# A sequence buffer in chunks of eight steps with permuted PSUM writes, and the encoder's output gate on ScalarE

## The reference

```
h = tok(x)                         # q, k, v = x@W + b; scores = q k^T; y = (gamma * scores) v @ Wo + bo
                                   # h = y if y >= 0 else 0.25 * y
n = layernorm(h)                   # (16, 1024, 64)
h_fwd = lstm(n @ Wf + bf, Uf)                  # last hidden state, 128 wide
h_bwd = lstm(n @ Wb + bb, Ub, reverse=True)
dec   = lstm(concat(h_fwd, h_bwd) @ Wd + bd, Ud, return_sequences=True)   # same input at every step
h = h + dec @ Wo + bo
h = h + experts(layernorm(h))      # 8 experts, the best 2 of each token, exact gelu
```

## Time and profile before

| | |
|---|---|
| median of 3 runs | 4055.97 us (4055.7 to 4057.27) |
| the profiled execution's own time | 4059.22 us |
| its span, first to last instruction | 4057.4 us |
| mean granted TensorE clock | 0.954 of full speed |
| PE busy | 3735.3 us, 92% |
| DVE busy | 3216.8 us, 79% |
| ACT busy | 1822.8 us, 45% |
| POOL busy | 86.1 us, 2% |

### The profile page before, as it was taken

One profiled execution on the slowest core, in us unless ns is written; L12 is line 12 of the kernel. 1 busy time (PEld: TensorE's weight loads), 2 busy tenths in 40 slices (PEclk: granted clock), 3 DMA queues, 4 the chain that ended last, 5 costly groups with the idle time before them and its releaser, 6 DMA issues. The chain is left out here.

```text
span 4057.4 us, 159902 instructions
## 1 busy us (share of the span) xinstructions
PE 3735.3 (92%) x59839; PEld 2527.7 (62%) x59839; DVE 3216.8 (79%) x23274; ACT 1822.8 (45%) x9834; POOL 86.1 (2%) x131
## 2 busy tenths in 40 slices
PE   6888799999999999999999799999998999899898
PEld 3222377777777777777777655655555555555564
DVE  5766699999999999999999766767666677666775
ACT  3333355555555555555555343434444343434443
POOL 6100000000000000000000000000000000000000
PEclk8888899999999999999999799999999999999999
DMA  3000000000000000000000000000000000000000
GB/s 88 16 21 16 14 3 3 3 3 3 3 3 3 3 4 3 3 4 3 3 3 4 5 6 6 8 7 7 6 7 6 7 7 7 7 6 6 7 7 7
DMA packets 49586, 33.99 MB, mean 8 GB/s; under 512 B 37661, under 2 KB 46877, under 8 KB 48806
## 3 DMA queue, kind: packets, MB, share of 16 engines
q1 hardware_dynamic: 48806, 23.77, 2.3%
HBM read 15.37 MB, written 8.39 MB: 6 GB/s over the span
## 5 line engine op out<-in xcount | busy, mean ns | idle before, releaser
L733 PE MATMUL bank<-xs,ident 128*128 128x128 f16 x13490 | 1202.4, 222 | 0.0
L733 PEld LDWEIGHTS bank<-xs,ident 128*128 128x128 f16 x13490 | 824.4, 98 | 60.5 <-issue 38.2
L742 PEld LDWEIGHTS bank<-enc_hi,u_lo 128*128 128x128 f16 x8192 | 350.3, 98 | 321.1 <-DVE enc_hi L788 311.5
L745 PE MATMUL bank<-enc_lo,u_hi 128*128 128x16 f16 x8192 | 529.9, 173 | 10.7 <-DVE enc_lo L794 8.9
L742 PE MATMUL bank<-enc_hi,u_lo 128*128 128x16 f16 x8192 | 532.9, 173 | 5.8 <-DVE enc_hi L788 4.5
L767 DVE SCALAR_TENSOR_TENSOR terms_dec<-ifg_cell_dec 128x32 f32<-128x32 f32 x1024 | 197.4, 193 | 417.6 <-ACT ifg_cell_dec L753 407.0
L753 ACT ACTIVATE ifg_cell_dec<-bank 128x48 f32<-128x48 f32 x1024 | 216.1, 211 | 659.4 <-PE bank L745 659.4
L742 PE MATMUL bank<-enc_hi,u_hi 128*128 128x16 f16 x8192 | 502.3, 170 | 0.0
L742 PEld LDWEIGHTS bank<-ring_hi,u_lo 128*128 128x128 f16 x4096 | 175.8, 97 | 484.7 <-DVE ring_hi L788 465.5
L742 PE MATMUL bank<-ring_hi,u_lo 128*128 128x16 f16 x4096 | 264.3, 173 | 183.7 <-DVE ring_hi L788 149.8
L745 PEld LDWEIGHTS bank<-enc_lo,u_hi 128*128 128x128 f16 x8192 | 341.6, 97 | 87.7 <-DVE enc_lo L794 16.8
(11 more groups left out here) (269 smaller groups left out, 7960.9 us busy)
## 6 DMA issues: line engine op xcount, KB each, us to landing
g_rows<-tok_d_gamma_batched_dram SPq DMA_DIRECT2D x8, 512.0 KB, 6.7
x_rows<-in_x_dram SPq DMA_DIRECT2D x16, 256.0 KB, 3.1
kept_h<-tok_ln_h SPq DMA_DIRECT2D x32, 128.0 KB, 2.0
res<-kept_h SPq DMA_DIRECT2D x32, 128.0 KB
out_dram<-sums SPq DMA_DIRECT2D x32, 128.0 KB
raw_wd<-in_L_attn_Wd_dram SPq DMA_DIRECT2D x2, 256.0 KB
raw_experts<-in_L_ffn_W_dram SPq DMA_DIRECT2D x2, 256.0 KB
raw_u<-in_L_attn_Uf_dram SPq DMA_DIRECT2D x1, 256.0 KB
```

The source lines that it names most:

```text
L733: nc.tensor.matmul(spare, m.ident16[:], m.xs[:, COLS:COLS + P], start=False, stop=True, skip_group_check=True)
L742: nc.tensor.matmul(z[k], w[:, g, :], h_hi, start=False, stop=False, skip_group_check=True)
L745: last = nc.tensor.matmul(z[k], m.u_hi[c.d][:, g, :], h_lo, start=False, stop=True, skip_group_check=True)
```

## The change

- `xs` becomes (chunk of 8 steps, batch, step) without pads, so that L582 writes runs of 8 steps (16 bytes) for its batch.
- A fill reads its 128 columns as one contiguous block still, now in the order (batch, step). To put them where they belong, its output in PSUM is addressed in the order (batch, step) too: `z.rearrange("p t b -> p b t")`.
- The encoder's output gate, (tanh(o) + 1) * 0.5 * scale, moves from DVE (L779) to ACT, as an Identity activation with scale and a bias from the tile `half_scale`, right behind the tanh of o. It waits for that tanh.
- DVE's waits for `s_out_gate` (ahead of `enc_hi`) and, in the encoder, for `s_cell` (ahead of `terms`) are dropped.
- `dve_rest` stays as it was for the decoder.

```diff
--- before.py
+++ after.py
@@ -107,7 +107,7 @@
         m.gT = sb("gammaT", [P, NB, T], F32)
 
 
-        m.xs = sb("xs", [P, T * B + 2 * COLS], F16)
+        m.xs = sb("xs", [P, CHUNKS, B, STEPS], F16)
         m.u_hi = [sb(f"u_hi{d}", [P, 4, H], F16) for d in range(3)]
         m.u_lo = [sb(f"u_lo{d}", [P, 4, H], F16) for d in range(3)]
         m.w_hi = [sb(f"w_hi{d}", [P, 4, H], F16) for d in range(2)]
@@ -240,8 +240,6 @@
                 nc.gpsimd.memset(m.bias[:], 0.0).then_inc(s_bz, 1)
                 nc.gpsimd.memset(m.ones3[:], Z_SCALE)
                 nc.gpsimd.memset(m.ones_s[:], MIX_SCALE ** 2)
-                nc.gpsimd.memset(m.xs[:, 0:COLS], 0.0)
-                nc.gpsimd.memset(m.xs[:, COLS + T * B:], 0.0)
 
             @block.tensor
             def _(pe):
@@ -579,8 +577,8 @@
                         S.activation(ln.split[:, :, 0:D], ln.square[:], ACT.Identity).then_inc(s_nh, 1)
                     if t == 13:
                         act.wait_ge(s_nT, b + 1)
-                        S.copy(m.xs[:, COLS:COLS + T * B].rearrange("p (t b) -> p t b", b=B)[:, :, b],
-                               m.bank[7][:].bitcast(F16)).then_inc(s_nk, 1)
+                        S.copy(m.xs[:, :, b, :], m.bank[7][:].bitcast(F16).rearrange("p (c t) -> p c t", t=STEPS)
+                               ).then_inc(s_nk, 1)
 
                 def prep(b, t):
                     k = b % 2
@@ -730,7 +728,7 @@
 def pe_idle(nc, m, spare, count):
 
     for _ in range(count):
-        nc.tensor.matmul(spare, m.ident16[:], m.xs[:, COLS:COLS + P], start=False, stop=True, skip_group_check=True)
+        nc.tensor.matmul(spare, m.ident16[:], m.xs[:, 0, :, :].rearrange("p b t -> p (b t)"), start=False, stop=True, skip_group_check=True)
 
 
 def pe_gates(nc, pe, m, c, n, h_hi, h_lo, ifg, o):
@@ -760,10 +758,11 @@
     nc.scalar.activation(c.tanh_cell, c.twice_cell[:], ACT.Tanh, scale=0.5).then_inc(c.s_tanh_cell, 1)
 
 
-def dve_terms(nc, dve, c, n):
+def dve_terms(nc, dve, c, n, own_cell=True):
 
     dve.wait_ge(c.s_t_ifg, n + 1)
-    dve.wait_ge(c.s_cell, n + 1)
+    if own_cell:
+        dve.wait_ge(c.s_cell, n + 1)
     nc.vector.scalar_tensor_tensor(c.terms[:], c.ifg_cell[:, 0:2, :], 1.0, c.ifg_cell[:, 2:4, :], ALU.add, ALU.mult
                                    ).then_inc(c.s_terms, 1)
 
@@ -773,13 +772,23 @@
     nc.vector.tensor_tensor(c.twice_cell[:], c.terms[:, 0, :], c.terms[:, 1, :], ALU.add).then_inc(c.s_twice, 1)
 
 
+def act_out_gate(nc, act, c, n, half_scale):
+    act.wait_ge(c.s_t_o, n + 1)
+    nc.scalar.activation(c.out_gate[:], c.tanh_o[:], ACT.Identity, scale=0.5 * X_SCALE, bias=half_scale
+                         ).then_inc(c.s_out_gate, 1)
+
+
+def dve_half_cell(nc, dve, c, sums):
+    dve.wait_ge(c.s_twice, sums)
+    nc.vector.tensor_scalar(c.ifg_cell[:, 3, :], c.twice_cell[:], 0.5, None, ALU.mult).then_inc(c.s_cell, 1)
+
+
 def dve_rest(nc, dve, c, n, sums):
 
     dve.wait_ge(c.s_t_o, n + 1)
     nc.vector.tensor_scalar(c.out_gate[:], c.tanh_o[:], 1.0, 0.5 * X_SCALE, ALU.add, ALU.mult
                             ).then_inc(c.s_out_gate, 1)
-    dve.wait_ge(c.s_twice, sums)
-    nc.vector.tensor_scalar(c.ifg_cell[:, 3, :], c.twice_cell[:], 0.5, None, ALU.mult).then_inc(c.s_cell, 1)
+    dve_half_cell(nc, dve, c, sums)
 
 
 def dve_hidden(nc, dve, c, n, h_hi):
@@ -805,6 +814,8 @@
         ch = [Chain(sb, sem, d, name, m.bank[6 + d]) for d, name in enumerate(("fwd", "bwd"))]
         s_set = sem("encoder_state_set")
         hello = sb("encoder_hello", [P, 1], F32)
+        half_scale = sb("encoder_half_scale", [P, 1], F32)
+        s_half_scale = sem("half_scale_set")
         h = list(zip(m.enc_hi, m.enc_lo))
 
 
@@ -824,13 +835,14 @@
 
                     g = SLOT_GATE[k]
                     z = banks[d][q % 2][:, :, k, :] if k < 3 else o_banks[d]
-                    first = COLS + STEPS * B * (CHUNKS - 1 - q if d else q)
-
-                    nc.tensor.matmul(z, m.w_hi[d][:, g, :], m.xs[:, bass.ds(first, STEPS * B)],
+                    z = z.rearrange("p t b -> p b t")
+                    x = m.xs[:, CHUNKS - 1 - q if d else q, :, :]
+
+                    nc.tensor.matmul(z, m.w_hi[d][:, g, :], x,
                                      start=(k in (0, 3)), stop=False, skip_group_check=True)
-                    nc.tensor.matmul(z, m.w_lo[d][:, g, :], m.xs[:, bass.ds(first, STEPS * B)],
+                    nc.tensor.matmul(z, m.w_lo[d][:, g, :], x,
                                      start=False, stop=False, skip_group_check=True)
-                    nc.tensor.matmul(z, m.lstm_bias[d][:, GATE_FROM[g], :], m.ones3[:],
+                    nc.tensor.matmul(z, m.lstm_bias[d][:, GATE_FROM[g], :], m.ones3[:].rearrange("p (b t) -> p b t", b=B),
                                      start=False, stop=False, skip_group_check=True)
 
                 for d in range(2):
@@ -858,26 +870,29 @@
             @block.scalar
             def _(act):
                 nc.scalar.activation(hello[:], m.ident[:, 0:1], ACT.Gelu)
+                act.wait_ge(s_half_scale, 1)
                 for n in range(T):
                     act_cell(nc, act, ch[1], n)
                     act_gates(nc, act, ch[0], n, *at(0, n))
+                    act_out_gate(nc, act, ch[0], n, half_scale[:])
                     act_cell(nc, act, ch[0], n)
                     act_gates(nc, act, ch[1], n, *at(1, n))
+                    act_out_gate(nc, act, ch[1], n, half_scale[:])
                 act_cell(nc, act, ch[1], T)
 
             @block.vector
             def _(dve):
                 own = Links(dve, s_set)
+                nc.vector.memset(half_scale[:], 0.5 * X_SCALE).then_inc(s_half_scale, 1)
                 for d in range(2):
                     ch[d].start(nc, own)
-                nc.vector.memset(ch[1].out_gate[:], 0.0).then_inc(ch[1].s_out_gate, 1)
+                own.link(nc.vector.memset(ch[1].out_gate[:], 0.0))
                 nc.vector.memset(h[0][0][:], 0.0).then_inc(ch[0].s_hi, 1)
                 nc.vector.memset(h[0][1][:], 0.0).then_inc(ch[0].s_lo, 1)
                 nc.vector.memset(ch[1].h[:], 0.0).then_inc(ch[1].s_twice, 1)
 
                 def hidden(late, n):
                     dve.wait_ge(ch[late].s_tanh_cell, n + 1)
-                    dve.wait_ge(ch[late].s_out_gate, n + 1)
                     dve_hidden(nc, dve, ch[late], n, h[late][0][:])
 
                 for n in range(T):
@@ -885,10 +900,10 @@
 
                         late = 1 - d
                         hidden(late, n)
-                        dve_terms(nc, dve, ch[d], n)
+                        dve_terms(nc, dve, ch[d], n, own_cell=False)
                         dve_hidden_low(nc, dve, ch[late], n, h[late][0][:], h[late][1][:])
                         dve_sum(nc, dve, ch[d], n)
-                        dve_rest(nc, dve, ch[d], n, n + 1 + d)
+                        dve_half_cell(nc, dve, ch[d], n + 1 + d)
                 hidden(1, T)
                 dve_hidden_low(nc, dve, ch[1], T, h[1][0][:], h[1][1][:])
 
```

## The result

The changed kernel takes 3966.41 us (median of 4 runs, 3961.21 to 3970.66) where the kernel before takes 4056.62 in the same set of runs: a ratio of 0.9766, 95% interval 0.9753 to 0.9778. It is 90 us faster. The profiled execution took 3965.94 us over a span of 3964.1, 93.3 us less than before.

What follows compares the result with a forecast made beforehand. Token mixing was held by the slow scattered copy on ACT, the encoder by its step order. Batches' 58.8 us plus 1.9 and 3.4 at the end, encoder 0, gave 64 off 4055.97: 3992 us, range 3974 to 4012.

Steps and rivals of the forecast that it cites:

- The copy's 1.01 us: Token mixing, ACT's L582: one copy into xs falls from 4.49 to 1.01 us, at most 1.46.
- the wait at the k tile: Token mixing: DVE's 3.52 us wait (L697) behind the slow copy shrinks, giving back 3.31 us a batch.
- rival 2: Token mixing: the gap shrinks but the clock falls all the same; 51.6 us gained, 4004 us; chance 0.10.
- the 0.89 us to `x_split`: Token mixing, from L697 to L685: 0.89 us a batch comes back if the clock stays full.
- the encoder's loop without L779: Encoder: the 0.85 us half-step loop closes without the gate instruction on DVE, so removing it gains 0.
- ACT's room for the new activation: Encoder, ACT: the moved gate takes 0.28 us, hidden with 0.08 to spare; above 0.36 it would hold L760.
- PE's slack for the fills: Encoder, PE: a fill of three matmuls may grow by 0.22 us, up to 0.07 each, and stay hidden.
- My value for the permuted fills: Encoder, PE: writing PSUM in permuted order costs 0 a matmul, spacing staying at 0.055 us.
- the 0.13: Encoder, PE: from a matmul spacing of 0.13 us on, each of 1024 fills delays its half step.
- The two dropped waits: Encoder, DVE: the waits on s_out_gate and s_cell were met long before, so dropping them gains 0.
- 4.20 us a batch: Token mixing: gain per batch from 3.31 and 0.89 us, over 14 batches 58.8 us.
- rival 4: Encoder: a thinner DVE queue lets something start earlier, 41 us more gained, 3951 us; chance 0.07.

Runs made afterwards that it cites:

- e1: Changed kernel with the output gate back on DVE and both dropped waits back; 3988.1 us, ratio 0.9819.
- e4: Kernel before with only each fill's bias matmul writing PSUM in the permuted order; 4062.21 us against 4062.18, ratio 0.9994.
- e7: Kernel before with its slow copy into xs one slot later, behind the k tile in ACT's queue; 4012.92 us, ratio 0.9883.
- x1: Changed kernel, gate still on ACT, with both dropped DVE waits back; 3978.75 us, ratio 0.9797.
- x2_shift3: Changed kernel with gate on DVE, s_out_gate wait back, s_cell wait still dropped, three more instructions ahead of DVE's loop; encoder 1746.3 us.
- x5: Changed kernel with the s_cell wait alone back; encoder 1742.2 us.
- x6: Changed kernel with the s_out_gate wait alone back; encoder 1745.5 us.
- x2_no_cell_wait: Changed kernel with gate on DVE and s_out_gate wait back, only the s_cell wait dropped; 3972.99 us, ratio 0.9784.
- x7: Kernel before with the s_cell wait alone dropped, gate still on DVE; 4043.42 us, ratio 0.9944.
- x2_shift1: Changed kernel with gate on DVE, s_out_gate wait back, s_cell wait still dropped, one more instruction ahead of DVE's loop; encoder 1739.1 us.
- the three shifts: Changed kernel with 1, 2 or 3 more instructions ahead of DVE's encoder loop; 3972.64, 3981.05 and 3985.36 us.
- e8: Changed kernel with xs in runs of 4 steps (8 bytes); 3975.02 us, one run.
- e9: Changed kernel with xs in runs of 2 steps (4 bytes); 3970.56 us, one run.
- x8: Changed kernel where DVE also makes the output gate into a tile nobody reads, its wait riding on the instruction; 3965.15 us, ratio 0.9759.
- e2: Kernel before with only the output gate moved to ACT and both waits dropped; 4040.13 us, ratio 0.995.
- e3: Changed kernel with fills reading xs permuted and writing PSUM in the old order; 4198.58 us, ratio 1.0349.
- x4_shift3: Changed kernel with three more instructions ahead of DVE's encoder loop; 3985.36 us.

## Why the prediction was wrong

**What held.** The copy's 1.01 us; the wait at the k tile; the clock that comes back with it (it is 0.51 behind the gap in the earlier trace rows; the mean up to the encoder goes from 0.86 to 0.96, and rival 2 is out); the 0.89 us to `x_split`; the encoder's loop without L779; ACT's room for the new activation, by 0.05 us (it takes 0.31, I had 0.28, and L758 would have been held from 0.36 on); no change of function table in the encoder's steps (the last `ACT_TABLE_LOAD` of the changed kernel, 1.28 us, is at 421.5 us, ahead of them); PE's slack for the fills. My value for the permuted fills, no cost per matmul, was wrong: L843 to L845 is 0.11 against 0.055 us. The fills before, whose runs of 16 leave gaps, are not slowed (0.055 too, as `pe_idle`'s contiguous ones). The 0.11 is under the 0.13 from which on I had a fill delay its half step, so the sum is the same. The jumps of the earlier trace rows every 16 columns said nothing about a jump at each.

**The step that failed:** "The two dropped waits (on `s_out_gate` and on `s_cell`) were met long before; 0 too." They were met, and they are worth 20.6 us. Of the encoder's late steps the traces show this:

- Waits of their own in DVE's loop, late steps at the border of each 128 instructions: 20.6 us of them in the kernel before, 19.4 in `e1`, 20.4 in `e4`, 20.7 in `e7`, 8.5 in `x1`, 13.2 in `x2_shift3`, 7.9 in `x5`, 7.0 in `x6`.
- Such waits and no step over 0.03 us too long: `x2_no_cell_wait` and `x7`, whose border is always on the halved cell, and `x2_shift1`, whose border is always on the gate.
- No such wait: none over 0.007 us in the changed kernel, the three shifts, `e8`, `e9` and `x8`, and one of 0.034 in `e2`. (`e3` has no such wait either, but its steps vary with the clock, 0.58.)

Why a wait of its own lets the border show was not shown by any run. The traces do show when the packets of the instruction queue (q14) start, taken between 600 and 2000 us. In every kernel with waits of their own, a packet most often starts 0.54 to 0.67 us after DVE starts the border's instruction (95 of 115 borders in the kernel before, within 0.2 us of each other). In the eight without, it starts 1.0 to 1.4 us before it (66 of 77 in the changed kernel). The two times are 1.5 to 2.1 us apart. It is 0.54 and 0.62 us after the border also in `x2_no_cell_wait`, `x7` and `x2_shift1`, which have no late step: their packets come as in the kernels with late steps, and only the place of the border differs. That the packet's time is what makes an instruction late is my guess; no run tests it. The decoder keeps both waits in all kernels. There, at the full clock, a step with a border takes 0.03 to 0.06 us longer than one without, with 81 borders some 2 to 5 us in all, an estimate. In the encoder a border cost up to 0.28 us of a step before and nothing in the changed kernel, where no step is over 0.004 us longer than the usual.

The late rows were in the trace before, as "issue" of 0.20 us and as 20 us between the step of 1.70 and the stretch's mean of 1.72, which I booked as clock: "most of the rest goes with the stretches behind its 0.97". `e1`, `e2` and `e4` show that this was wrong: the late steps stay when the clock is 1.00, and the clock itself accounts for 2 us at most.

**A term mis-sized:** 4.20 us a batch. Twelve batches from the second copy on came 27.22 us apart and now come 22.33, so 4.89. "From L685 on, DVE runs without a gap, so nothing later takes the gain away" missed the `q_lo` wait, 1.42 and now 0.79 us: PE was, as I read it, still behind from its stretch at the lower clock (0.51 in the earlier trace rows). `e7` bears this out: `q_lo` waits 0.79 us in its batches at full clock, and 1.52 in those behind a fall of the clock, the first of them that at 175.6 us. 3.40 + 0.89 + 0.63 = 4.92. That is 8 us over 12 batches. Between the first two copies only 0.2 us were gained, 4 less than the sum has. I put that down to GpSimd's work on the weights: `x_split` at 88.60 has GpSimd busy for 2.54 of its 2.61 us, while with an idle GpSimd, from 124.97 us on, it takes 0.69. With 1.2 us more from the first batch, the last one and the end, the stage comes to 69.6 in place of the sum's 64.

**Not settled:** the 7 us between a step of 1.700 and one of 1.693. `e7`, whose encoder code is that of before, has 1.694; `e1`, `e2`, `e4`, `x2_shift1`, `x6`, `x7` and `x8` have 1.700, the changed kernel, the shifts and the rest (but `e3`) 1.692 to 1.695. No edit goes with it. So rival 4, an encoder that gains too, came closest to the cause, but by another mechanism than the one it names.

## What to carry to other kernels

A wait that is always met was not free where it stood in DVE's queue as an instruction of its own (7.0 to 20.7 us of late steps in eight kernels): look for small "issue" gaps that come at a fixed count of instructions, and let program order or a wait that rides on an operation do the work (`x8`: no late step). A stage's mean step against its usual step shows such losses; find the long steps before giving them a cause. The slow copy cost what was queued behind it on ACT (DVE's 3.52 us at the k tile, gone in `e7` with a copy of 4.53 us), and a layout is chosen with the price of each side: here side-by-side pairs of f16 were enough for ACT's writes (1.03 us a copy against 4.49), scattered PSUM writes one behind the other doubled the spacing of matmuls of 128 columns (0.11 against 0.055 us), and a scattered read made it four times as long (0.21).

## What the runs showed of the hardware

- ACT's copy of 128x1024 f16: 4.49 us with single elements 32 bytes apart, 1.03 us in runs of 4 bytes, 1.01 in runs of 8 and of 16.
- A PE matmul of 128 columns: 0.055 us apart with output in runs of 16 f32, 0.11 with each output column in a place of its own (0.06 to 0.07 behind the first or only such one), 0.21 with one f16 read every 16 bytes, and this last at the lower clock (0.5) too, where the contiguous one takes 0.107 (`e3`).
- The page's instruction queue has 312 packets before and 280 after, for 159902 and 155805 instructions: 128 instructions a packet. One instruction of DVE in 128, always the same, came up to 0.31 us late in the encoder's loop with waits of their own, and in the eight kernels without no step was over 0.034 us too long.
- The decoder's code is the same in all kernels, yet it takes 1794.6 us at a granted clock of 0.98 (`e4`), 1805.5 at 0.96 and 1824.1 at 0.94 (`x4_shift3`). That makes most of the 10 to 20 us between executions of kernels that should be equal. The encoder at 0.97 and at 1.00 takes nearly the same (1759.7 and 1759.3 us).
- An Identity activation of 128x16 with a bias from a tile takes 0.31 us; the tanh of the same size without one 0.18.
